# A graph kernel in two passes: tiles of z made in another order and kept later, and z of a half tile put in its bank ahead of the product

## The reference

```python
# layer 0
msg = relu(x[src] + edge_attr)
agg = segment_sum(msg, dst)
h = x + (x + agg)
f = gelu(bn1(h) @ W1.T + b1) @ W2.T + b2
x = layernorm(x + bn2(h + f))
# layer 1
h = gelu((x[src] + edge_attr) @ W1m + b1m)
agg = segment_sum(h @ W2m + b2m, dst) / max(deg, 1)
u = gelu(agg @ W1u + b1u) @ W2u + b2u
x = layernorm(x + (layernorm(x + u) * gamma + beta))   # layer norm of layer 1 inside
```

## Time and profile before

| | us |
|---|---|
| median of 3 runs | 2683.39 (2683.18 to 2701.86) |
| profiled execution, its own time | 2682.52 |
| its span in the profile | 2680.7 |
| first pass, from about 56 to about 1258 in the span | 1202 |
| second pass, from about 1340 to about 2640 | 1300 |

### The profile page before, as it was taken

How to read it: one execution, slowest core, us unless ns; L and a number is a source line. 1 busy time by engine, 2 the same in 40 slices (tenths; PEclk the granted TensorE clock), 3 DMA queues, 4 the chain that set the end, 5 groups by cost and what they waited for, 6 DMA issues and landing times.

```text
span 2680.7 us, 37644 instructions
## 1 busy us (share of the span) xinstructions
PE 2069.6 (77%) x9200; PEld 1692.6 (63%) x9200; DVE 1472.3 (55%) x3240; ACT 1304.0 (49%) x2684; POOL 1621.7 (60%) x1672
## 2 busy tenths in 40 slices
PE   3688777887788777778458888788788888788886
PEld 2566666666566666666346666666666666666665
DVE  3355554555545545455234665665666665665665
ACT  4555555555555555556134444444444444444543
POOL 6666666666666666662456666566566666666640
PEclk8989989898988888999768888888889898898988
DMA  7788878888888788886456666666566666666651
GB/s 219 241 265 271 268 255 263 268 265 266 256 274 262 260 272 259 273 259 198 140 145 183 176 179 184 177 181 181 174 180 188 177 181 175 185 186 183 190 162 40
DMA packets 347272, 567.03 MB, mean 212 GB/s; under 512 B 47994, under 2 KB 213494, under 8 KB 347206
## 3 DMA queue, kind: packets, MB, share of 16 engines
q1 hardware_dynamic: 266972, 347.29, 41.7%
q0 software_dynamic: 79872, 218.21, 26.6%
q10 hardware_dynamic: 362, 0.85, 0.1%
HBM read 499.67 MB, written 66.49 MB: 211 GB/s over the span
## 4 chain that ended last, share of the span: by engine, by line
PE 36%; another core or an unknown queue 22%; issue 15%; ACT 14%; DVE 10%; DVEq 2%; ACTq 1%
PE bank L828 13%; PE bank L770 6%; PE bank L795 4%; ACT m_all L542 4%; ACT bank L538 3%; PE bank L845 3%; DVE m_lo L1079 3%; PE bank L742 2%; PE bank L752 2%; PE bank L684 2%; ACT bank L570 2%; DVE bank L1074 1%; ACT m_hi L569 1%; DVEq L1033 1%
## 5 line engine op out<-in xcount | busy, mean ns | idle before, releaser
L410 POOL DMA_INDIRECT m_all<-y_scratch,src_u x832 | 807.9, 971 | 555.0 <-DVE bank L1074 263.2
L410 POOL DMA_INDIRECT m_all<-in_x,src_p x816 | 796.9, 977 | 412.1 <-issue 214.5
L828 PE MATMUL bank<-w1m_sb,e_all 128*128 128x256 f32 x2080 | 625.7, 444 | 221.3 <-DVE m_lo L1079 135.3
L828 PEld LDWEIGHTS bank<-w1m_sb,e_all 128*128 128x128 f32 x2080 | 433.4, 220 | 315.7 <-issue 128.6
L770 PE MATMUL bank<-m_all,sel 128*128 128x257 f32 x1664 | 482.8, 421 | 123.9 <-ACT m_all L542 102.9
L1074 DVE TENSOR_TENSOR bank<-bank,m_all 128x512 f32<-128x512 f32 x416 | 289.4, 696 | 406.0 <-remote 151.3
L770 PEld LDWEIGHTS bank<-m_all,sel 128*128 128x128 f32 x1664 | 341.9, 211 | 215.2 <-ACT m_all L542 122.6
L795 PE MATMUL bank<-w1m_sb,ez 128*128 128x256 f32 x1248 | 353.8, 409 | 152.2 <-issue 100.4
L569 ACT ACTIVATE m_hi<-bank 128x512 fp32r<-128x512 f32 x416 | 248.2, 597 | 345.7 <-DVE bank L1074 111.8
L795 PEld LDWEIGHTS bank<-w1m_sb,ez 128*128 128x128 f32 x1248 | 241.3, 203 | 201.0 <-issue 171.7
L845 PE MATMUL bank<-m_lo,sel 128*128 128x256 f32 x832 | 302.3, 385 | 45.0 <-issue 23.6
(11 more groups left out here) (129 smaller groups left out, 2055.3 us busy)
## 6 DMA issues: line engine op xcount, KB each, us to landing
e_all<-in_edge SPq DMA_DIRECT2D x416, 256.0 KB
e_all<-in_edgeT SPq DMA_DIRECT2D x208, 256.0 KB
ez<-in_edgeT SPq DMA_DIRECT2D x104, 384.0 KB
z_scratch<-zc SPq DMA_DIRECT2D x104, 384.0 KB
e_all<-z_scratch SPq DMA_DIRECT2D x104, 256.0 KB
e_all<-in_edgeT SPq DMA_DIRECT2D x104, 128.0 KB
e_all<-z_scratch SPq DMA_DIRECT2D x104, 128.0 KB
m_all<-y_scratch,src_u POOLq DMA_INDIRECT x832
```

The costliest lines, as they stand in the source:

```text
L410: pool.indirect_dma_start(out=m_sb[n % ROUND][:, t, :], out_offset=None, in_=table, in_offset=bass.IndirectOffsetOnAxis(ap=sources(g, u), ...
L828: last = pe.matmul(z_bank(s)[:, t * D:(t + 1) * D], eT_sb[s % ERING][:, k, t * P:(t + 1) * P], w1m_sb[:, k, :], start=(k == 0), stop=(k == ...
```

## The change: what it does

In the first pass PE makes the tiles of `z` in the order 2, 0, 1. Tile 2 is made at the start of step j = 1, tile 0 at the end of j = 2, tile 1 at the start of j = 3. ACT copies tile 2 at j = 3 (now `keep_one`), and tiles 0 and 1 at j = 1 of the next group (`keep_two`), after `copy_sums` of j = 0. SP's load of the columns moves from j = 0 to j = 1 of its own loop, and its condition is now that tiles 0 and 1 are made. The store waits for `keep_two`. In the second pass `put_z` no longer waits for the product; instead the product of j = 2 waits for `put_z` of the same bank. What is computed does not change, nor does the number of instructions that compute or transfer. Its core:

```diff
-                if j == 0 and 1 <= g < G - 1:
-                    sp.wait_ge(z_ahead, g)
+                if j == 1 and 1 <= g < G - 1:
+                    sp.wait_ge(z_two, g)
                     sp.dma_start(ez_sb[(g + 1) % 2][:], edge_columns(g + 1, TILES - AHEAD, TILES)
                                  ).then_inc(ez_in[(g + 1) % 2], 16)
                 if j == 3 and 1 <= g <= G:
-                    sp.wait_ge(z_kept, g)
+                    sp.wait_ge(kept_two, g)
                     sp.dma_start(z_dram[g - 1], zc_sb[(g - 1) % 2][:]).then_inc(z_out[(g - 1) % 2], 16)
...
-            def keep_two(i, q):
-
-                act.wait_ge(z_ahead0, PER_ROUND * i + q + 1)
+            def keep_one(i, q):
+
+                act.wait_ge(z_one, PER_ROUND * i + q + 1)
                 if not (known(i) and PER_ROUND * i + q < 2):
                     act.wait_ge(z_out[q % 2], 32 * i + 16 * (q // 2))
-                act.copy(zc_sb[q % 2][:, 0:2 * D], ahead_bank[0][:]).then_inc(z_kept0, 1)
-
-            def keep_third(i, q):
-                act.wait_ge(z_ahead, PER_ROUND * i + q + 1)
-                act.copy(zc_sb[q % 2][:, 2 * D:3 * D], ahead_bank[1][:, 0:D]).then_inc(z_kept, 1)
+                act.copy(zc_sb[q % 2][:, 2 * D:3 * D], ahead_bank[1][:, 0:D]).then_inc(kept_one, 1)
+
+            def keep_two(i, q):
+
+                act.wait_ge(z_two, PER_ROUND * i + q + 1)
+                act.copy(zc_sb[q % 2][:, 0:2 * D], ahead_bank[0][:]).then_inc(kept_two, 1)
...
                 lo = D if s % PAIRS == 2 else 0
-                if lo:
-                    act.wait_ge(z_made, 3 * (PER_ROUND * i + s // PAIRS) + 3)
                 act.copy(z_bank(s)[:, lo:2 * D], e_all[:, s % ERING, lo:2 * D]).then_inc(z_put, 1)
...
+                if s % PAIRS == 2:
+
+                    pe.wait_ge(z_put, 2 * (PER_ROUND * i + s // PAIRS) + 1)
                 for t in range(2 if s % PAIRS < 2 else 1):
...
-                    if j != 1:
-                        ahead(i, q, max(j - 1, 0))
+                    if j == 1:
+                        ahead(i, q, 2)
+                    if j == 3:
+                        ahead(i, q, 1)
                     sums(i, s)
+                    if j == 2:
+                        ahead(i, q, 0)
```

More of the change, by code:

```diff
@@ L227, in build @@
         ez_in, z_out = sems("ez_in", 2), sems("z_out", 2)
-        z_ahead0, z_ahead, z_kept0, z_kept, z_put = map(sem, ("z_ahead0", "z_ahead", "z_kept0", "z_kept", "z_put"))
+        z_two, z_one, kept_two, kept_one, z_put = map(sem, ("z_two", "z_one", "kept_two", "kept_one", "z_put"))
         e_moved = sem("e_moved")
@@ L587, in first_pass @@
                 if j == 3 and (not known(i) or PER_ROUND * i + q < G):
-                    keep_two(i, q)
+                    keep_one(i, q)
                 before = (i, q - 1) if q else (i - 1, PER_ROUND - 1)
@@ L591, in first_pass @@
                     if j == 0:
-                        keep_third(*before)
                         copy_sums(0, *before)
+                    if j == 1:
+                        keep_two(*before)
                 if known(i) and i == 0:
@@ L617, in relu_general @@
                     relu(i, PAIRS * q + j)
+                keep_one(i, q)
                 keep_two(i, q)
-                keep_third(i, q)
             def gelu_general(i, q):
@@ L788, in ahead @@
             def ahead(i, q, a):
-                if a == 0:
+                if a == 2:
                     pe.wait_ge(ez_in[q % 2], ez_used(i, q))
                 if a != 1 and not (known(i) and PER_ROUND * i + q < 1):
-                    pe.wait_ge(z_kept if a else z_kept0, PER_ROUND * i + q)
+                    pe.wait_ge(kept_one if a else kept_two, PER_ROUND * i + q)
                 for k in range(KD):
@@ L798, in ahead @@
                 if a:
-                    last.then_inc(z_ahead if a == AHEAD - 1 else z_ahead0, 1)
+                    last.then_inc(z_one if a == 2 else z_two, 1)
             def sums(i, s):
@@ L878, in sums_general @@
             def sums_general(i, q):
-                for a in range(AHEAD):
+                for a in (2, 0, 1):
                     ahead(i, q, a)
@@ L893, in banks_left @@
                 pe.wait_ge(a_yr, C)
-                pe.wait_ge(z_kept, G)
+                pe.wait_ge(kept_one, G)
+                pe.wait_ge(kept_two, G)
             with pe.If(is_general > 0):
```

1 line of the change is left out of this document (added).

## The result

The changed kernel took 2701.03 us (median of 11 runs, 2690.19 to 2706.14), the kernel before 2685.07 (11 runs beside them). The ratio is 1.0045, interval [1.0024, 1.0066]: 0.45% slower, where 2630 us was forecast.

A forecast was written before the change was run, and what follows sets the result against it. The prediction took both passes as loops of waits between PE, ACT and DVE. Its terms, -59 - 38 + 44 = -53 us, from 2682.5 gave 2630 us; 8-in-10 range 2565 to 2725, forecast's own 2595 to 2665.

The forecast's parts named there:

- The first pass, -59 us: First pass: 12.6 and 28.9 us saved in 72.5 groups, 59 us for 104; ends 0 and 162 us.
- In the other 38.5 groups PE was held by the copy of two tiles: First pass: PE idle there at most 2.6 us a group; 0.75 us taken as gain, 28.9 us in all.
- the removed copy of the third tile: First pass: this 0.37 us copy no longer stands ahead of `copy_sums`; in 34 groups it saves 12.6 us.
- The low end: First pass: PE's idle before z tiles gives no gain if `copy_sums` then holds PE as long.
- PE has sums and the turn of the group to do there, so it costs nothing.: First pass: copy of two tiles, 0.585 us, ahead of the third step's relu is free; without cover 61 us.
- SP's edits at nothing: First pass: moving SP's load of columns and the store's wait costs nothing; eight buffers of edge rows cover it.
- Second pass, -38 + 44 = +6 us: Second pass: 38 us gained as ACT's gelu stops waiting for the product; 44 us lost as the product waits for ACT.
- The rule against the change: If PE works past its modelled end, its real idle is 0.73 us, not 3.51; first pass gains 27 us at most.
- The figure of 27 us: First pass: most it gains if PE was still at work after its modelled end, the 28.9 us falling to about 6.
- PE is the bound: Rival, chance 0.30: 27 us at most gained in first pass, some 8 against 44 lost in second; 2692 or about 2670 us.
- The new wait decides: Rival, chance 0.20: second pass, PE stops at `z_put` in one group of four, losing 117 us; 2740 us.
- The waits were the whole of it: Rival, chance 0.12: PE's idle before z tiles goes entirely, 144 us, against +26 us in the second pass; 2565 us.

The follow-up runs named there:

- the recorded pair: The kernel before and the changed kernel with both parts, all gathers in place, as first compared and profiled: 2685.07 and 2701.03 us.
- place 2685: Circumstance, not a changed kernel: where the unchanged kernel took 2685 us (2686 in three later experiments); the runs do not say what differs.
- place 2231: Circumstance, not a changed kernel: where the unchanged kernel took 2228 to 2233 us, as beside all experiments but three.

## Why the prediction was wrong, step by step

**What bounds the kernel.** I read loops of waits between PE, ACT and DVE, as no engine was full. That was half right. But ACT's 4.7 us of waits a group were no proof of a loop: with z tiles made twice ACT waits 274.5 us in 76 groups, 3.6 us a group, while PE never stops. In the recorded pair itself PE did have idle time, 2.46 us a group, so there something more than PE's work set the pace.

**The first pass, -59 us: the step that failed.** "In the other 38.5 groups PE was held by the copy of two tiles" (28.9 us) and the removed copy of the third tile (12.6 us) were both priced as time off the path. The first was also misread: of the 100.4 us the row puts only 44.1 down to that copy, and 56.0 to no wait that shows. The waits did go, as forecast (ACT below 1 us a group, PE at 4.3 us, under the 30 I had named), but the sum of PE's idle stayed, 178 and 184 us, since `copy_sums` took all of it over. The low end, "the least is nothing, if `copy_sums` then holds it as long", came nearest. The term measured +20.2 us in 80 groups, +23.4 from the first relu to the last, and a loss was not in its range.

**"PE has sums and the turn of the group to do there, so it costs nothing."** The second failing step. I named the cover and its price, 61 us, but had not seen that the change takes part of that cover away. Before, tile 1 stood ahead of the sums of the third step; now no tile does, since tile 0 is made only behind them. And this is the very place where ACT has the longer chain, `copy_sums`, relu, `keep_two`, relu. The runs price both together at 0.27 us a group with half of the gathers (28 us in 104 groups) and 0.17 with tiles made twice; the recorded pair lost 20.2 / 80 = 0.25. The place of the tile alone gave back 17.0 of 21.6 and 13.5 of 13.5 us. That it is the cause in the recorded pair too is inferred from the like size and not shown; it wasn't tried with all gathers in place 2685. One rival stands there: PE's late releases, counted below, now fall on `copy_sums`, with the next relu and PE's sums behind it, where they fell on the z copies.

**SP's edits at nothing.** No wait of ACT or DVE for an edge row shows after the change; right.

**Second pass, -38 + 44 = +6 us.** The measured -2.3 us in 80 groups is close, but the terms aren't shown separately. The mechanism was right, the new wait on PE behind a late `put_z`: 189.0 us in 1150, 2.05 us a group where I had named 1 to 2. Its price depends on what else binds: nothing in the recorded pair, 27.1 us in 80 groups with half of the gathers. With all of them in place 2231 it is small and not settled. The edit alone was 0.45% slower, but the whole change, which contains it, had the ratio 1.0003; the steady second pass took 818.7 to 825.3 us in three profiles with the edit and 812.1 to 818.5 in seven with the second pass of before. That an earlier copy cures it shows that the cost was the place of the copy in ACT's order, not that PE waits in place of ACT.

**The rule against the change.** In place 2231 and with half of the gathers, ACT's copy of the sums, where ACT waited for it, starts 0.04 us (median) after the modelled end of the last sums. So the modelled end is good in those runs, and it is likely that the releases 1 to 8 us late in the recorded pair are really late; for that pair itself no run shows it. The Trainium skill, page "Perfetto Trace Analysis", section "Summary: the profiler window per engine type", calls that end an estimate with the actual end hidden; here the measurement confines the error to about 0.1 us outside the recorded pair. The figure of 27 us that I derived from it was nearer to the truth than 59, but still a gain where there was a loss, and not for the reason given.

**The rivals.** "PE is the bound", with `copy_sums` taking over ACT's wait in full (2683 us), came nearest: it had ACT's idle moving to `copy_sums`, though the first pass then did not stay as it was but grew by 23.4 us. I gave that 2683 without a sum; with nothing in the first pass and +6 in the second it would be 2688. "The new wait decides" (2740) was wrong, though the wait did appear where it said. "The waits were the whole of it" is ruled out. That the range, 2565 to 2725, held the 2701 was luck: all its slow side was the second pass, while the loss was in the first.

**Still open** is what makes place 2685 slower by a fifth. Its mark are PE's late releases: of ACT's waits of over a quarter of a microsecond before `copy_sums` in groups 20 to 103, 19 of 32 ended more than 1 us after the modelled end in the kernel before and 44 of 62 in the changed one, none in place 2231. With half of the gathers in place 2685 it was 1 of some 130 in three kernels, and their steady parts were as fast as in place 2231. So the lateness goes with the full number of gathers there. Whether the gathers cause it, or a PE that waits often, as in the recorded pair at a granted clock of 0.88 against 0.97 for the three, isn't settled: the kernels that would tell, with tiles made twice, all ran in place 2231.

## What to carry to other kernels

In these runs idle time before a copy that waits for a full or nearly full engine was slack, not cost; removing the wait moved it to the next thing that needs that engine. Before work is moved out from under a wait, look at what it covers where it stands and what chain will then have no cover, on the engine that feeds and not only on the one that waits. And take the suspected bound away in an experiment (half of the gathers, tiles made twice): it made a 0.45% question one of 3.1%, and showed that the two orders differ in the opposite sense from the forecast.

## What the runs showed of the hardware

The same program took 2685 us in one place and 2231 in another, with granted clocks of TensorE of 0.88 and 0.96. The gathers of its first pass took the same 0.98 us each in both. Twelve records of matmuls a group more, 263 us of busy time, cost 47 us in place 2231, where POOL's gathers bound the kernel; PE was then granted 1.00 over 800 us without a gap, against 0.98 in the same stretch of the kernel without them.
